# A binary convolution on TensorE: the last images in half-image tiles

## The reference

```
g   = (x - mean) / sqrt(var + 1e-5)        # per image and group of 8 channels
A   = M*M + sum_k(Z_k*Z_k) / 100
w   = M / sqrt(A) + sum_k rv_k * Z_k / sqrt(A)      # 256 x 256 x 3 x 3
out = x + alpha * conv3x3(sign(g), sign(w), padding 1)   # alpha per output channel
```

## Time and profile before

| | |
|---|---|
| median of 3 runs | 524.27 us (523.59 to 525.61) |
| profiled execution, its own time | 522.31 us |
| its span | 520.5 us |
| mean granted TensorE clock | 0.981 of full speed |
| PE busy, DVE busy, ACT busy | 482.7, 375.4, 328.8 us |
| DMA | 124.37 MB, mean 239 GB/s |

### The profile page before, as it was taken

The page is one execution under the profiler, slowest core; times in us unless marked ns, Lnnn a source line. Parts: engine busy times, 40 slices in busy tenths (PEclk is TensorE's granted clock), DMA queues, the critical chain, the costliest instruction groups (busy, mean ns, idle before and its releaser), DMA issues.

```text
span 520.5 us, 8289 instructions
## 1 busy us (share of the span) xinstructions
PE 482.7 (93%) x2794; PEld 401.2 (77%) x2794; DVE 375.4 (72%) x711; ACT 328.8 (63%) x566; POOL 22.8 (4%) x70
## 2 busy tenths in 40 slices
PE   0898969899999999999999999999999999999990
PEld 0454637788888888888888888888888888888880
DVE  1122458757977978878879879879779779776656
ACT  0787766577667667676676676676676766754320
POOL 8200000000000000000000000000000000000000
PEclk9999997989999999999999999999999999999996
DMA  6999958018568578568568568568577577544226
GB/s 235 399 396 396 397 216 345 0 63 309 214 220 307 191 243 276 211 243 290 191 242 287 195 241 295 191 241 292 197 251 273 210 261 268 202 148 186 87 100 247
DMA packets 45644, 124.37 MB, mean 239 GB/s; under 512 B 3632, under 2 KB 3632, under 8 KB 45616
## 3 DMA queue, kind: packets, MB, share of 16 engines
q1 hardware_dynamic: 45616, 124.01, 65.8%
HBM read 72.62 MB, written 51.38 MB: 238 GB/s over the span
## 4 chain that ended last, share of the span: by engine, by line
PE 86%; DVE 4%; DMA 3%; ACT 2%; SPq 2%; issue 2%; DVEq 0%; ACTq 0%
PE conv_ps L353 80%; DMA m_sb<-in_L_conv_M_dram 3%; SPq L245 2%; PE conv_ps L294 2%; ACT whole L409 1%; DVE x_sb L699 1%; PE conv_ps L307 1%; DVE bn L623 1%; PE conv_ps L297 1%; PE conv_ps L311 1%; PE grp_ps L337 1%; DVE low L605 0%; ACT signs L459 0%; DVE whole L673 0%; ACT low L414 0%
## 5 line engine op out<-in xcount | busy, mean ns | idle before, releaser
L353 PE MATMUL conv_ps<-signs,wts 128*128 128x492 f32 (+5 forms) x1926 | 425.5, 381 | 2.4 <-ACT signs L459 2.1
L353 PEld LDWEIGHTS conv_ps<-signs,wts 128*128 128x128 f32 x1926 | 361.6, 190 | 59.0 <-ACT signs L459 2.5
L467 ACT ACTIVATE part<-conv_ps 128x492 int32<-128x492 f32 (+3 forms) x107 | 61.4, 574 | 147.0 <-PE conv_ps L353 147.0
L459 ACT ACTIVATE signs<-x_sb,shift,rstd 128x784 fp32r<-128x784 f32 x128 | 125.8, 1035 | 0.8 <-DVE shift L660 0.8
L673 DVE SCALAR_TENSOR_TENSOR whole<-conv_ps,part 128x492 int32<-128x492 f32 (+3 forms) x107 | 70.9, 663 | 73.5 <-PE conv_ps L353 65.2
L681 DVE SCALAR_TENSOR_TENSOR low<-whole,conv_ps 128x492 f32<-128x492 int16 (+3 forms) x107 | 70.5, 659 | 3.7
L699 DVE SCALAR_TENSOR_TENSOR x_sb<-whole,alpha_sb,x_sb 128x784 f32<-128x784 int16 x64 | 66.0, 1031 | 0.7
L699 DVE SCALAR_TENSOR_TENSOR x_sb<-low,alpha_sb,x_sb 128x784 f32<-128x784 f32 x64 | 65.9, 1029 | 0.0
L642 DVE BATCH_NORM_STATS2 bn<-x_sb 128x6 f32<-128x392 f32 x116 | 59.7, 557 | 0.8 <-issue 0.6
L437 ACT ACTIVATE unread<-x_sb 128x784 bf16<-128x784 f32 x58 | 49.2, 848 | 0.0
L439 ACT ACTIVATE unread<-x_sb 128x784 bf16<-128x784 f32 x58 | 49.1, 847 | 0.0
(11 more groups left out here) (46 smaller groups left out, 150.5 us busy)
## 6 DMA issues: line engine op xcount, KB each, us to landing
x_sb<-in_x_dram SPq DMA_DIRECT2D x64, 784.0 KB, 5.7
out_dram<-x_sb SPq DMA_DIRECT2D x64, 784.0 KB, 3.8
x_sb<-in_L_conv_Z_dram SPq DMA_DIRECT2D x64, 288.0 KB, 7.4
m_sb<-in_L_conv_M_dram SPq DMA_DIRECT2D x8, 288.0 KB, 8.3
alpha_sb<-in_L_conv_alpha_dram SPq DMA_DIRECT2D x2, 0.5 KB, 2.4
rv_sb<-in_L_conv_rv_dram SPq DMA_DIRECT2D x1, 4.0 KB, 2.4
```

The lines of the kernel that those rows point to most:

```text
L353: mm = pe.matmul(sums_of_tile(b, skip, drop), wts[:, ch, kh * KW + kw], e, start=n == 0, stop=n == PRODUCTS - 1, skip_group_check=True)
L459: nc.scalar.activation(o, x_sb[:, slot_of(t, j), h].rearrange("p (a b) -> p a b", b=W), ACT.Sign, bias=shift[:, t % BODY, j, h:h + 1], sca ...
L467: nc.scalar.activation(part[:, bank(b), 0:columns(b)], conv_ps[bank(b)][:, 0:columns(b)], ACT.Copy, scale=-FRACTION / PACK, bias=FRACTION ...
```

## The change

The last body now ends after four triples. The last triple and image 63 (called END and ONE) are done after it as eight tiles: two for each of the four images, each of 14 rows (14 x 29 = 406 columns), in image order. The bank is the tile's number in this list, modulo five. TensorE's order (first of tile i, rest of tile i - 1) stays. VectorE does, after each tile's two sums, the outputs of that tile's 14 rows of the image. What was left of the triple before (two tiles, the outputs of its three images) and the statistics of image 63 are placed in between. SP stores images 60, 61 and 62 whole, as before; image 63 is stored in two DMAs of half an image each, the first after a new semaphore `rows_done`.

```diff
-            body(BODIES - 1, BODY + 1, False, True)
+            body(BODIES - 1, BODY, False, True)
...
-            return TOP_PIX if b < TRI else TRI * SIDE_PIX[b - TRI] if b < TILES else REST
+            return TOP_PIX if b < TRI else TRI * SIDE_PIX[b - TRI] if b < TILES else HALF_SPAN
...
+        END, ONE = BODY, BODY + 1
+        LAST = tuple((END, TILES + i) for i in range(2 * TRI)) + ((ONE, TILES), (ONE, TILES + 1))
+        BEFORE = (TRIPLES - 1) * TRI * HALVES
+        LAST_TILE = (TRIPLES - 1) * TILES
...
+            if b >= TILES:
+                j, half = divmod(b - TILES, 2)
+                return v[:, j, half * HALF_SPAN + skip:(half + 1) * HALF_SPAN - drop]
...
-            store(BODIES - 1, BODY + 1, 0)
+            for j in range(TRI):
+                sp.wait_ge(out_done, BEFORE + (j + 1) * HALVES)
+                store_rows(END, j, 0, H)
+            sp.wait_ge(rows_done, HALVES)
+            store_rows(ONE, 0, 0, H // 2)
+            sp.wait_ge(out_done, N * HALVES)
+            store_rows(ONE, 0, H // 2, H)
...
@@ tensor @@
-            number = TRIPLES * TILES
-            first_products(TRIPLES, BODY + 1, 0, 1, number)
-            rest_products(BODY, TILES - 1, number - 1)
-            first_products(TRIPLES, BODY + 1, TILES, 1, number + 1)
-            rest_products(BODY + 1, 0, number)
-            rest_products(BODY + 1, TILES, number + 1)
+            for i, (t, b) in enumerate(LAST):
+                images = N if t == ONE else N - TRI + (b - TILES) // 2
+                first_products(t, b, i % TILES, images, LAST_TILE + i)
+                if i == 0:
+                    group(TRIPLES + 1, ONE, 0, 1, N)
+                t, b = LAST[i - 1] if i > 0 else (END - 1, TILES - 1)
+                rest_products(t, b, (i - 1) % TILES, LAST_TILE + i - 1)
+            rest_products(ONE, TILES + 1, (len(LAST) - 1) % TILES, LAST_TILE + len(LAST) - 1)
...
@@ scalar @@
-            fraction(0, TRIPLES * TILES)
-            fraction(TILES, TRIPLES * TILES + 1)
+            for i, (t, b) in enumerate(LAST):
+                fraction(b, i % TILES, LAST_TILE + i)
+                if i == 0:
+                    copy_group(TRIPLES + 1, ONE, 0, 1)
+                if i == 1:
+                    deviation(TRIPLES + 1, ONE, 0, 1)
+                if i == 2:
+                    image_signs(TRIPLES, TRIPLES + 1, ONE, 0)
...
@@ vector @@
-            end = TRIPLES * TILES
-            for b in (TRI, TRI + 1):
-                tile_sums(TRIPLES - 1, BODY, b, end - TILES + b)
-            outputs(BODY, 0, end)
-            tile_sums(TRIPLES, BODY + 1, 0, end)
-            outputs(BODY, 1, end)
-            tile_sums(TRIPLES, BODY + 1, TILES, end + 1)
-            outputs(BODY, 2, end)
-            outputs(BODY + 1, 0, end + 2)
+            tile_sums(TRIPLES - 2, END - 1, TRI, TRI, LAST_TILE - 2)
+            tile_sums(TRIPLES - 2, END - 1, TRI + 1, TRI + 1, LAST_TILE - 1)
+            outputs(END - 1, 0, LAST_TILE, out_done)
+            bounded(TRIPLES + 1, ONE, 0, 1)
+            for i, (t, b) in enumerate(LAST):
+                k, end = TRIPLES - 1 + t - END, LAST_TILE + i + 1
+                tile_sums(k, t, b, i % TILES, LAST_TILE + i)
+                if i == 0:
+                    outputs(END - 1, 1, LAST_TILE, out_done)
+                    negative_mean(TRIPLES + 1, ONE, 0, 1)
+                if i == 1:
+                    outputs(END - 1, 2, LAST_TILE, out_done)
+                j, half = divmod(b - TILES, 2)
+                if half == 0:
+                    outputs(t, j, end, rows_done if t == ONE else None, 0, H // 2)
+                else:
+                    outputs(t, j, end, out_done, H // 2, H)
```

More of the change, by code:

```diff
@@ L56, in conv_preact @@
     REST = SPAN - 1 - MIDDLE
+    HALF_SPAN = SPAN // 2
     SIDE_PIX = (REST // 2 + 1, REST // 2 - 1)
-    assert REST % 4 == 2 and TOP_PIX % 2 == 0 and TRI * SIDE_PIX[0] <= 512 and TOP_PIX <= 512
+    assert REST % 4 == 2 and HALF_SPAN % PITCH == 0 and TOP_PIX % 2 == 0 and TRI * SIDE_PIX[0] <= 512 and TOP_PIX <= 512
     SLOTS = TRI * BODY
@@ L177, in conv_preact @@
         out_done = sem("out_done")
+        rows_done = sem("rows_done")
         def need(eng, s, value):
@@ L280, in _, with store_rows @@
             bodies(sp, body)
-            store(BODIES - 1, BODY + 1, 0)
+            def store_rows(t, j, r0, r1):
+                n = (BODIES - 1) * SLOTS + TRI * t + j
+                sp.dma_start(out_v[n][:, :, r0 * W:r1 * W],
+                             x_sb[:, slot_of(t, j), :, r0 * W:r1 * W]).then_inc(stored[slot_of(t, j)], 16)
+            for j in range(TRI):
[5 more added lines that the diff above has]
+            store_rows(ONE, 0, H // 2, H)
             for n in range(SLOTS):
-                sp.wait_ge(stored[n], 16 * len(range(n, N, SLOTS)))
+                sp.wait_ge(stored[n], 16 * (len(range(n, N, SLOTS)) + (1 if n == slot_of(ONE, 0) else 0)))
         @block.tensor
@@ L339, in group, with products @@
                           stop=True).then_inc(grp_done, 1)
-            def products(t, b, n0, n1):
+            def products(t, b, at, n0, n1):
                 for n in range(n0, n1):
@@ L346, in products, with first_products, rest_products @@
                     kh = ROW_ORDER[row]
-                    skip = W if kh == 0 and b < TRI else 0
-                    drop = W if kh == KH - 1 and b >= TRI + 1 else 0
+                    skip = W if kh == 0 and (b < TRI or b >= TILES and (b - TILES) % 2 == 0) else 0
+                    drop = W if kh == KH - 1 and (b == TRI + 1 or b >= TILES and (b - TILES) % 2 == 1) else 0
                     shift_by = kh * PITCH + kw
-                    e = image_tile(signs[:, t % 2 * TRI:(t % 2 + 1) * TRI, ch, shift_by:shift_by + SPAN - 1], b, skip,
+                    e = image_tile(signs[:, t % 2 * TRI:(t % 2 + 1) * TRI, ch, shift_by:shift_by + SPAN], b, skip,
                                    drop)
-                    mm = pe.matmul(sums_of_tile(b, skip, drop), wts[:, ch, kh * KW + kw], e, start=n == 0,
+                    mm = pe.matmul(sums_of_tile(b, at, skip, drop), wts[:, ch, kh * KW + kw], e, start=n == 0,
                                    stop=n == PRODUCTS - 1, skip_group_check=True)
                 return mm
-            def first_products(k, t, b, signed, number):
-                pe.wait_ge(signs_done, (k * TRI + signed) * HALVES)
+            def first_products(t, b, at, images, number):
+                pe.wait_ge(signs_done, images * HALVES)
                 need(pe, low_done, number - TILES + 1)
-                products(t, b, 0, SPLIT).then_inc(first_done, 1)
-            def rest_products(t, b, number):
+                products(t, b, at, 0, SPLIT).then_inc(first_done, 1)
+            def rest_products(t, b, at, number):
                 pe.wait_ge(part_done, number + 1)
-                products(t, b, SPLIT, PRODUCTS).then_inc(rest_done, 1)
+                products(t, b, at, SPLIT, PRODUCTS).then_inc(rest_done, 1)
             pe.wait_ge(const_step, CONST_STEPS)
@@ L461, in image_signs, with fraction @@
                                          scale=rstd[:, t % BODY, j, h:h + 1]).then_inc(signs_done, 1)
-            def fraction(b, number):
+            def fraction(b, at, number):
                 act.wait_ge(first_done, number + 1)
                 need(act, whole_done, number - TILES + 1)
-                nc.scalar.activation(part[:, bank(b), 0:columns(b)], conv_ps[bank(b)][:, 0:columns(b)], ACT.Copy,
+                nc.scalar.activation(part[:, at, 0:columns(b)], conv_ps[at][:, 0:columns(b)], ACT.Copy,
                                      scale=-FRACTION / PACK, bias=FRACTION / 2).then_inc(part_done, 1)
@@ L502, in body @@
                         if start and b == 0:
-                            fraction(0, 0)
+                            fraction(0, 0, 0)
                             image_signs(0, 1, 0, 2)
@@ L508, in body @@
                             sums(r, t + STAT_LEAD, j)
-                        fraction(b, k * TILES + b)
+                        fraction(b, b, k * TILES + b)
                         if b == (3 if start else 0):
@@ L577, in _ @@
             bodies(pool, body)
+            variance(TRIPLES + 1, ONE, 0, 1)
         @block.vector
@@ L666, in high, with high_sum, low_sum @@
                 return v.bitcast(I16)[..., 1::2]
-            def high_sum(k, t, b, number):
+            def high_sum(k, t, b, at, number):
                 dve.wait_ge(rest_done, number + 1)
                 need(dve, out_done, (k - 1) * TRI * HALVES)
-                fractions = part[:, bank(b), 0:columns(b)].bitcast(U16)[:, 0::2]
+                fractions = part[:, at, 0:columns(b)].bitcast(U16)[:, 0::2]
                 nc.vector.scalar_tensor_tensor(out=image_tile(whole[:, t % 2], b),
-                                               in0=flat_tile(conv_ps[bank(b)][:, 0:columns(b)], b),
```

(15 more changed lines are left out.)

28 lines of the change are left out of this document (12 added, 16 removed).

## The result

The changed kernel took 517.62 us (median of four runs, 517.31 to 518.57) against 524.37 (four runs, 523.59 to 525.61): a ratio of 0.988, 95% interval 0.985 to 0.990. Two later comparisons, of six runs each, gave 519.42 against 523.73 (0.992, 0.990 to 0.994) and 519.33 against 523.83 (0.991, 0.989 to 0.994). Over all of them the medians are 519.1 (16 runs) and 523.8 (49 runs). The forecast was 519.4, the range 517.6 to 521.2.

The account below looks back on a forecast made before the run. TensorE was taken to set the time, with leftover vector work and the last store making the end. Vector work 3.9 us plus store 1.1, less 0.1 for waits, gave 4.9 off 524.27: 519.4 us, range 517.6 to 521.2.

Parts of the forecast that it names:

- the wait of "at worst 0.1": Before the last tile's rest, TensorE might wait for ScalarE's fraction, at worst 0.1 us, off the path.
- the signs of being wrong: Changed profile: half outputs at 0.7 or more, no idle before tile 6, TensorE waiting, or last store's data for 2 us.
- VectorE's prices: VectorE's instructions in the half tiles: sum 0.575 us, half output 0.59 (0.51 to next start), half tile with outputs 2.23.
- Rival (b): Half tiles on VectorE: small pieces as dear as large, 0.70 us each; only 1.7 to 2.7 us less; 8 in 100.
- (c): Last eight tiles: VectorE becomes the bound, half outputs 0.96 us; kernel 1.5 to 2.5 us slower; 3 in 100.
- The order: VectorE in the last tiles: idle before tiles 5 and 6, then two half tiles left, ending 3.86 us earlier.
- Rival (a): Kernel's end: only one half tile trails TensorE, 6.5 us less in all, 517.8 us; 5 in 100.
- The store: Last store, half of image 63 instead of a whole image: 1.13 us of data, 1.1 us saved.
- The sum: Whole kernel: 3.9 us plus 1.1 from the last store, less 0.1 for small waits: 4.9 us less.

Follow-up runs that it names:

- early_rest: The changed kernel with TensorE doing the rest of tile 6 after five matmuls of tile 7 instead of fourteen; 518.25 us, ratio 0.990.
- whole_store: The changed kernel with image 63 stored by one DMA of 784 KB after its last output; 520.03 us over five runs, ratio to before 0.993.

## Why the prediction was right

**TensorE.** Forecast 0.07 us more, found 0.17 to 0.18 in all three profiles. A column cost the same in tiles of 406: the fractions after are 3.26 us apart, as worked out. The last rest started late, since ScalarE's fraction came just too late: the wait of "at worst 0.1". Of the last four matmuls the second starts 0.29 us after the first, and the later ones 0.17 to 0.18 apart; early_rest, where the brackets show the wait for the fraction, has the same 0.29. This 0.1 and the 0.07 of columns make up the 0.18. TensorE waiting for `part` stands among the signs of being wrong; it did show, at a size that decides nothing.

**VectorE's prices.** A sum of 406: 0.577 against 0.575. A half output: 0.62 to 0.63 and 0.54 to the next, against 0.59 and 0.51. The price was taken from the sums and from a statistics instruction. The whole output's own row would have been nearer: 1.03 less 392 elements at the sums' 1.09 ns is 0.60. With both sizes on record an output costs 1.04 ns an element and a fixed 0.21 us, where a sum has 0.14; why was not tried. A half tile takes 2.31, not 2.23. What matters is that it stays under 3.26. Rival (b)'s 0.70 is 0.07 above what was found, (c)'s 0.96 far above.

**The order.** VectorE idle before tiles 5 and 6: 0.83 and 0.89 us, as described (worked out: 1.2 and 1.0). Two half tiles after the rest of tile 6, because of the two rests: VectorE ends 3.88 us after T, forecast 3.88 (512.55 - 508.67). That this agrees so well is two misses that cancel: the two half tiles took 0.16 more than worked out, and VectorE could start them 0.81 us before T (508.25 against 509.06) and not 0.66, because of TensorE's wait in between. Rival (a), 6.5 less by the end alone, did not happen, though the first median looked like it; early_rest shows that the pair of rests is what stood between (3.88 to 2.43).

**The store.** Forecast 1.1, found 1.03 between the kernels (4.14 to 3.11) and 0.95 by the experiment; its data took 1.21, not 1.13. The stores of images 60 and 61 start at 497.07 and 501.68; the prediction put them one tile later, which costs nothing.

**The sum.** 4.78 against 4.9. By parts, in rounded figures: 3.94 of vector work left after T (7.82 to 3.88) and 1.03 of store, less 0.18 of TensorE. What I did not see is how much of a single comparison is scatter. The prediction gave it about 1 us; four runs of each kernel were off by 2. So the first median, 517.62, lies 1.8 below the forecast, outside the forecast's own range (518.3 to 520.6), and only 0.02 inside the stated one, whose lower end had been drawn for rival (a), which did not happen. That this median fell within the range is luck; what bears the prediction out is the clean measure and the two later medians, 519.42 and 519.33.

**The two rules of the Trainium skill.** The Trainium skill, "VectorE: DVE Perf Modes", section on the TRN2 errata, gives for an f32 add of two tensors what makes an estimate of 0.58 for the sum and 0.57 for the output. The sum agrees (0.577), the output does not (0.62). Its advice of 512 elements or more did not decide here, as VectorE had slack; the fixed part behind it is in the rows (0.14 us a sum). The Trainium skill, "DMA: Bandwidth & Descriptors", section on the anatomy of one DMA, gives a fit of 2.0 us and the bytes at 436 GB/s for DMAs issued from GpSimd; here SP issues them. By it the estimates are 2.9 us for a half store and 3.8 for a whole one. From issue to landing the profiles show 2.5 (changed) and 3.4 (whole_store), so the fixed part is 0.4 less here, and the difference of 0.9 agrees.

## What to carry to other kernels

At the end of a kernel count what is left on each engine when the slowest one stops, and cut the last work so that this is one small piece and one small store. Where the last two tiles are finished by a pair of steps, the second engine gets both at once. Before a step is moved ahead, ask what it covered where it was: here that gave back half of the gain, and once it was mended the next engine's backlog took most of the rest. And measure a change of 1% from an instruction that both kernels share, not from the start of the span.

## What the runs showed of the hardware

Every profile has the same stop of TensorE early in the convolution, 2.46 us from one matmul's start to the next (it waits for ScalarE's signs). In six of eleven profiles the granted clock fell to the 1.2 GHz level for 3.4 us, some 3 to 4 us after the stop began; in five it did not, with either kernel, before and changed, in both groups. The stretch with the fall in the changed kernel's second profile, then the same stretch in its first:

```profile
104.50:108.40 3.90, 1.83 (x9) 1.27 (x8) 2.76 (x7) 3.67 (x6) 0.00 (x0) 1.00 0.00 0
108.40:111.80 3.40, 3.40 (x11) 2.82 (x10) 0.00 (x0) 3.40 (x6) 0.00 (x0) 0.50 0.00 0
```

```profile
103.00:106.90 3.90, 1.83 (x8) 1.25 (x8) 2.76 (x7) 3.67 (x6) 0.00 (x0) 1.00 0.00 0
106.90:110.30 3.40, 3.40 (x18) 3.01 (x17) 0.46 (x1) 3.40 (x6) 0.00 (x0) 1.00 0.00 0
```

In 3.4 us 11 matmuls run instead of 18. The granted clock is at the lower level, too, when the first wide matmul (the first of the convolution) starts. From the five profiles of the two kernels, in us:

| profile | first wide matmul starts | lower level from there on | of this the fall | first wide matmul to T |
|---|---|---|---|---|
| before | 81.0 | 6.3 | 3.4 | 427.6 |
| before, again | 83.7 | 5.5 | 0 | 427.2 |
| changed | 82.0 | 4.7 | 0 | 427.1 |
| changed, second | 83.7 | 7.7 | 3.4 | 428.4 |
| changed, third | 83.0 | 5.1 | 0 | 427.3 |

So it is not the fall alone that counts, but all the time at the lower level: half of what one profile has more of it, 1.5 us for the second of the changed kernel against the first and 0.4 for the kernel before, is near the measured 1.3 and 0.4. The start of the first wide matmul goes with the clock as well: four of the eleven profiles show an earlier fall of 3.4 us, at 50 to 52 us, and there it starts at 82.9 to 83.7, in the other seven at 81.0 to 82.0. Its start and the time at the lower level together make the 1 to 3 us by which the spans of one kernel's profiles differ. Why the clock falls in one execution and not in another was not tried, and stays open.
